# Edge lists loaded by GpSimd, counting one chunk sooner, and head 0 aggregated ahead of head 1's last chunk, in a two-block graph-attention kernel

## The reference

```python
edge_index = jnp.stack([src, dst])                       # 4096 edges among 256 nodes
x = _layernorm(x + _L0_gnn_ref(x, edge_index, ...))      # block 0: two GAT layers, 8 heads of 768, then 1 of 768
x = _layernorm(x + _L1_gnn_ref(x, edge_index, ...))      # block 1: two GAT layers, 4 heads of 256, then 1 of 768, with layer norms

# one GAT layer, self-loops appended to src and dst
h = (x @ W).reshape(n, heads, out_ch)
e = leaky_relu(alpha_src[src] + alpha_dst[dst], 0.2)     # alpha = <h, a> of each head
p = exp(e - segment_max(e, dst)[dst])
alpha = p / segment_sum(p, dst)[dst]
out = segment_sum(h[src] * alpha, dst) + b
```

## Time and profile before

| | |
|---|---|
| median of 3 runs | 353.04 us (353.0, 353.04, 353.94) |
| the profiled execution | 353.03 us |
| its span in the profile | 351.2 us |
| PE busy with matmuls | 343.7 us, 98% |
| DVE, ACT, POOL busy | 214.4 us (61%), 219.0 us (62%), 249.4 us (71%) |
| chain that ended last | PE 93%, DVE 4%, DMA 1% |

### The profile page before, as it was taken

How to read it: one execution, slowest core, us unless ns; L and a number is a source line. 1 busy time by engine, 2 the same in 40 slices (tenths; PEclk the granted TensorE clock), 3 DMA queues, 4 the chain that set the end, 5 groups by cost and what they waited for, 6 DMA issues and landing times.

```text
span 351.2 us, 6049 instructions
## 1 busy us (share of the span) xinstructions
PE 343.7 (98%) x2049; PEld 297.0 (85%) x2051; DVE 214.4 (61%) x543; ACT 219.0 (62%) x383; POOL 249.4 (71%) x165
## 2 busy tenths in 40 slices
PE   7999999999999999999999999999999999999994
PEld 4888989889988988988898898889777888888883
DVE  4999873354527327354541834464797899964776
ACT  5988597547736854773775486479585865444601
POOL 2479769576693965769397486959757899697911
PEclk9999999999999999999999999999999999999999
DMA  8887968475747547575754757654563557355002
GB/s 256 302 303 214 404 214 264 178 207 163 233 131 238 158 135 239 135 242 145 213 179 136 223 179 240 212 179 145 171 202 104 204 177 216 119 174 184 2 0 90
DMA packets 24833, 65.95 MB, mean 188 GB/s; under 512 B 1984, under 2 KB 3056, under 8 KB 24816
## 3 DMA queue, kind: packets, MB, share of 16 engines
...
...
## 4 chain that ended last, share of the span: by engine, by line
PE 93%; DVE 4%; DMA 1%; issue 0%; ACT 0%; DVEq 0%
PE ps L1098 65%; PE ps L1200 10%; PE ps L1495 10%; PE ps L1550 2%; PE ps L1166 2%; DMA x_sb<-in_x 1%; PE ps L1293 1%; PE ps L1151 1%; DVE stats L1944 1%; PE ps L1229 1%; DVE ps L2201 1%; PE ps L1434 1%; DVE z L2208 1%; PE ps L1573 0%; PE ps L1251 0%
## 5 line engine op out<-in xcount | busy, mean ns | idle before, releaser
L401 POOL TENSOR_TENSOR ring_lo<-raw,ring_hi 128x768 fp32r<-128x768 f32 x92 | 167.2, 1851 | 65.1 <-ACT ring_hi L388 65.0
L388 ACT ACTIVATE ring_hi<-raw 128x768 fp32r<-128x768 f32 x96 | 77.3, 839 | 33.8 <-PE ps L1098 28.5
L1098 PE MATMUL ps<-ring_hi,zT_hi 128*128 128x256 f32 (+1 forms) x256 | 69.8, 345 | 0.0
L1098 PE MATMUL ps<-ring_lo,zT_hi 128*128 128x256 f32 (+1 forms) x256 | 67.8, 338 | 0.0
L1098 PE MATMUL ps<-ring_hi,zT_lo 128*128 128x512 f32 (+1 forms) x256 | 67.5, 338 | 0.0
L417 POOL TENSOR_TENSOR ring_lo<-raw,ring_hi 128x512 fp32r<-128x512 f32 (+1 forms) x40 | 59.4, 1519 | 10.3 <-ACT ring_hi L410 10.3
L1712 DVE CUSTOM_DVE_ANT_0 e<-ps,att 128x768 f32<-128x768 f32 x36 | 32.4, 954 | 46.7 <-PE ps L1098 46.7
L1098 PE MATMUL ps<-ring_hi,xT_hi 128*128 128x512 f32 (+1 forms) x192 | 51.2, 340 | 0.0
L1098 PE MATMUL ps<-ring_hi,xT_lo 128*128 128x512 f32 (+1 forms) x192 | 50.7, 337 | 0.0
L1098 PE MATMUL ps<-ring_lo,xT_hi 128*128 128x512 f32 (+1 forms) x192 | 50.5, 337 | 0.0
L1098 PEld LDWEIGHTS ps<-ring_lo,zT_hi 128*128 128x128 f32 x256 | 43.3, 188 | 5.6
...
## 6 DMA issues: line engine op xcount, KB each, us to landing
...
```

Source lines behind the costliest of these rows:

```text
L388: eng.activation(slot_hi(c), raw_chunk(c), ACT.Copy).then_inc(hi_done, 1)
L401: eng.tensor_tensor(slot_lo(c), raw_chunk(c), slot_hi(c).bitcast(F32), ALU.subtract)\
L1098: last = pe.matmul(ps[:, at + to:at + to + hi - lo], a, b[:, lo:hi], start=start and n == 0 and to != D, stop=stop and n == PASSES - 1, sk ...
```

## The change

Eight edits. (1) Both edge lists are loaded by DMAs of POOL's own queue, behind its `iota`, which now comes first there; SP no longer loads them. (2) `zeros` and `half` are set by DVE and not by POOL. (3) DVE makes the edge numbers and the five early ramps ahead of chunk 0's low part. (4) `count_edges` and `scores(0)` stand before chunk 1 of phase 1, `weights(0)` half-way through chunk 4, and `aggregate_T(0)` before chunk 5; ACT makes its last ramps sooner, ahead of the high parts of chunks 2 to 5. (5) The two clearing matmuls go: the first accumulating matmuls open the banks. (6) In head 0's ELU, DVE takes head 1's dots behind the second third, and ACT does the last two chunks of phase 2 and head 1's first h_hi ahead of the last third's zT_hi. (7) The transposes of x1 are handed over in parts of two and four blocks; the matmul on `zeros` behind them goes. (8) DVE centres the second part of y's tile 1 behind x1's first two low parts.

```diff
--- before.py
+++ after.py
@@ -220,8 +220,8 @@
         GAT2_NAT_AT = [2 * BANK, 0]
         GAT2_WT_AT = [3 * BANK + N, BANK + N]
         R2_AT = 4 * BANK
-        X1T_AT = [(3 * BANK, 2 * BANK), (5 * BANK, 6 * BANK)]
-        X1T_PARTS = [4, KD]
+        X1T_AT = [(2 * BANK, 3 * BANK), (6 * BANK, 5 * BANK)]
+        X1T_PARTS = [2, KD]
         H1_PART = KH // 2
         ELU_AT = [2 * BANK, 6 * BANK, 7 * BANK]
         AM_AT = [T_AT, S_AT + N]
@@ -605,8 +605,6 @@
 
             sp.dma_start(raw[:, 0, 0:D], w1[:, 0, 0, :]).then_inc(single_loaded[0], 16)
             sp.dma_start(raw[:, 0, D:2 * D], w1[:, 1, 0, :]).then_inc(raw_full[0], 16)
-            sp.dma_start(edges[:, 0, :], src.rearrange("(p t) -> p t", p=P)).then_inc(edges_loaded, 16)
-            sp.dma_start(edges[:, 1, :], dst.rearrange("(p t) -> p t", p=P)).then_inc(edges_loaded, 16)
             load_x(1)
             sp.dma_start(raw[:, 1, 0:D], w1[:, 2, 0, :]).then_inc(single_loaded[1], 16)
             load_x(2)
@@ -646,13 +644,13 @@
 
         @block.gpsimd
         def _(pool):
-            pool.memset(zeros[:, :], 0.0).then_inc(zeros_set, 1)
-            pool.memset(half[:, :], -0.5).then_inc(half_set, 1)
+            pool.iota(iota_i, pattern=[[1, 1 + N]], base=-1, channel_multiplier=0).then_inc(iota_ready, 1)
+            for n, ends_of in enumerate((src, dst)):
+                pool.dma_start(edges[:, n, :], ends_of.rearrange("(p t) -> p t", p=P)).then_inc(edges_loaded, 16)
             pool.memset(ident[:, :], 0.0).then_inc(consts, 1)
             pool.wait_ge(consts, 1)
             pool.affine_select(out=ident[:, :], in_=ident[:, :], compare_op=ALU.not_equal, fill=1.0,
                                base=0, pattern=[[-1, P]], channel_multiplier=1).then_inc(consts, 1)
-            pool.iota(iota_i, pattern=[[1, 1 + N]], base=-1, channel_multiplier=0).then_inc(iota_ready, 1)
             pool.memset(stats[:, :, :, 12:15], 0.0).then_inc(eps_set, 1)
             pool.wait_ge(eps_set, 1)
             for n, width in enumerate((D, HC, D, D)):
@@ -925,12 +923,10 @@
 
             for c in (0, 1):
                 split_hi(act, 1, c)
-            steps(10, 14)
+            steps(10, 17)
             projected_hi(0)
-            for c in (2, 3):
-                split_hi(act, 1, c)
-            steps(14, ACT_STEPS)
-            for c in (4, 5):
+            steps(17, ACT_STEPS)
+            for c in (2, 3, 4, 5):
                 split_hi(act, 1, c)
             act.wait_ge(counted, 1)
             act.activation(step_sums, ps[:, STEPS_AT:STEPS_AT + 1 + N], ACT.Copy).then_inc(sums_copied, 1)
@@ -952,10 +948,13 @@
                 split_hi(act, 2, c)
             weights_hi(0)
             act.wait_ge(b1_ready, 2)
-            elu(0, between=lambda: projected_after_dots(1, 0))
-            split_hi(act, 2, 4)
+            def behind_last_exp():
+                for c in (4, 5):
+                    split_hi(act, 2, c)
+                projected_after_dots(1, 0)
+
+            elu(0, between=behind_last_exp)
             leaks(1)
-            split_hi(act, 2, 5)
             projected_after_dots(1, 1)
             exps(1, (1, 0))
             after_exps(1)
@@ -1088,7 +1087,7 @@
             def pieces(i):
                 return ((0, BANK, 0), (BANK, D, BANK)) if i == 0 else ((0, N, D), (N, D, 2 * BANK))
 
-            def product(at, i, lhs_hi, lhs_lo, w_hi, w_lo, start, stop, piece=None, passes=ALL):
+            def product(at, i, lhs_hi, lhs_lo, w_hi, w_lo, start, stop, piece=None, passes=ALL, opens=False):
 
                 last = None
                 for n, (a, b) in enumerate(three(lhs_hi, lhs_lo, w_hi, w_lo)):
@@ -1096,7 +1095,7 @@
                         continue
                     for lo, hi, to in pieces(i) if piece is None else pieces(i)[piece:piece + 1]:
                         last = pe.matmul(ps[:, at + to:at + to + hi - lo], a, b[:, lo:hi],
-                                         start=start and n == 0 and to != D,
+                                         start=n == 0 and (opens or start and to != D),
                                          stop=stop and n == PASSES - 1, skip_group_check=True)
                 return last
 
@@ -1294,28 +1293,22 @@
                 last.then_inc(counted, 1)
 
             for c in range(CH):
-                if c == 2:
+                if c == 1:
                     pe.wait_ge(b1_ready, 2)
                     count_edges()
                     scores(0)
-                project_chunk(1, 1, c, between=(lambda: weights(0)) if c == CH - 1 else None)
-
-            def clear_acc(b):
-                pe.matmul(ps[:, ACC + b * BANK:ACC + (b + 1) * BANK], zeros[:, 0:P], zeros[:, :],
-                          start=True, stop=False, skip_group_check=True)
-
-            aggregate_T(0)
-            clear_acc(1)
-            clear_acc(2)
-
-            def first_accumulate(c, i, passes=ALL, piece=None, start=False):
+                if c == CH - 1:
+                    aggregate_T(0)
+                project_chunk(1, 1, c, between=(lambda: weights(0)) if c == CH - 2 else None)
+
+            def first_accumulate(c, i, passes=ALL, piece=None, start=False, opens=False):
                 return product(ACC, i, node_tile(zT_hi, c, i), node_tile(zT_lo, c, i), slot_hi(c), slot_lo(c),
-                               start, False, passes=passes, piece=piece)
+                               start, False, passes=passes, piece=piece, opens=opens)
 
             pe.wait_ge(z_hi_done, 1)
             for c in (0, 1):
                 chunk(2, c)
-                first_accumulate(c, 1, passes=FIRST_TWO)
+                first_accumulate(c, 1, passes=FIRST_TWO, opens=c == 0)
             pe.wait_ge(z_lo_done, 1)
             for c in (0, 1):
                 first_accumulate(c, 1, passes=LAST_ONE)
@@ -1481,7 +1474,6 @@
                         last.then_inc(x1T_ps, 1)
 
             transpose_x1(0)
-            keep_warm(1, PROJ)
 
             def wide_product(q, at, i, passes=ALL):
 
@@ -1521,7 +1513,7 @@
                 wide_product(q, 0, 0, passes=LAST_ONE)
             for i in range(NT):
                 for q in w1a[2:] if i == 0 else w1a:
-                    if i == 0 and q["k"] == X1T_PARTS[0]:
+                    if i == 0 and q["k"] == BANK // P:
                         transpose_x1(1)
                     if q["k"] == X1T_PARTS[0] or i == 1 and q["k"] == 0:
                         pe.wait_ge(x1T_lo_done, 2 * i + 1 + (q["k"] > 0))
@@ -1637,6 +1629,8 @@
                 dve.tensor_tensor(xT_lo[:, 2 * b:2 * b + 2, :], of, xT_hi[:, 2 * b:2 * b + 2, :].bitcast(F32),
                                   ALU.subtract).then_inc(xT_lo_done, 1)
 
+            dve.memset(zeros[:, :], 0.0).then_inc(zeros_set, 1)
+            dve.memset(half[:, :], -0.5).then_inc(half_set, 1)
             dve.wait_ge(iota_ready, 1)
             dve.tensor_copy(iota[:, :], iota_i).then_inc(iota_cast, 1)
             dve.tensor_copy(iota_ps, iota_i).then_inc(iota_cast, 1)
@@ -1656,8 +1650,6 @@
                     dve.tensor_scalar(hot(t), iota_ps[:, 1:1 + P], row_of[:, t:t + 1], weight_of[:, t:t + 1], ALU.is_equal, ALU.mult)\
                        .then_inc(hot_done, 1)
 
-            split_lo(dve, FIRST_PHASE, 0)
-            input_lo(0)
             dve.wait_ge(edges_loaded, 32)
             dve.tensor_copy(edges_f[:, :, :], edges[:, :, :]).then_inc(edges_cast, 1)
             dve.wait_ge(edges_cast, 1)
@@ -1674,10 +1666,12 @@
                     dve.tensor_scalar(step(t), numbers, edges_f[:, 0, t:t + 1], weight_of[:, t:t + 1],
                                       ALU.is_lt if t >= BELOW_FROM else ALU.is_ge, ALU.mult).then_inc(step_dve_done, 1)
 
-            split_lo(dve, FIRST_PHASE, 1)
             dve.wait_ge(iota_cast, 2)
             dve.wait_ge(edges_split, 5)
             late_steps(ACT_STEPS, ACT_STEPS + STEPS_EARLY)
+            split_lo(dve, FIRST_PHASE, 0)
+            input_lo(0)
+            split_lo(dve, FIRST_PHASE, 1)
             split_lo(dve, FIRST_PHASE, 2)
             input_lo(1)
             late_steps(ACT_STEPS + STEPS_EARLY, ET - STEPS_LAST)
@@ -1846,9 +1840,9 @@
             def elu(h, between=None):
 
                 for q in range(3):
-                    if q == 1 and between is not None:
+                    if q == 2 and between is not None:
                         between()
-                    if q >= 1:
+                    elif q >= 1:
                         elu_lo(h, q - 1)
                     dve.wait_ge(elu_exp, 3 * h + q + 1)
                     for c in range(2):
@@ -1909,10 +1903,14 @@
             normalised(FIRST_HEAD, (0, 1))
             projected_lo(0, 1)
             weights_lo(0)
-            dve.wait_ge(att_loaded, 32 * 2)
-            dots(1, a_s, 0, a_src_done)
-            dots(1, a_d, 1, a_dst_done, tiles=(0,))
-            elu(0, between=lambda: dots(1, a_d, 1, a_dst_done, tiles=(1,)))
+            def next_dots():
+                dve.wait_ge(att_loaded, 32 * 2)
```

(8 more changed lines are left out.)

## The result

The changed kernel takes **360.63 us** (median of 5 runs, 360.49 to 360.70) against 353.36 us of the kernel before in the same comparison (5 runs, 353.0 to 354.75): 1.020 times as long, 95% interval 1.018 to 1.022. The forecast was 353.1 us with a range up to 355.0, so it missed by 7.5 us, on the side of its rival (b).

The account below looks back on a forecast made before the run. PE, working in 98% of the span, was taken as the bound. Opening and counting +0.94, accumulation gap -0.49, head 1's dots +0.15 and x1 -0.55 gave +0.05, 353.1 us; expected within 352.2 and 354.0, full range 351.8 to 355.0.

Parts of the forecast that it names:

- rival (b): Opening: edges come late through slow descriptor writing by POOL, PE waits for the first low part; 355.0 us, chance 0.22.
- the landing time: Opening: POOL's edge loads land at 4.6 us, so PE goes on at 7.80 instead of 7.17, +0.63 us.
- late end: Opening: edges land no sooner than SP's second edge load, 4.7 us after an issue at 2.11: 6.8 us.
- delay of some tenths: Opening: DVE's memsets and casts, under 1 us in all, stretch POOL's edge issues by some tenths of a us.
- early end: Opening: after POOL's iota and two issues of about 0.4 us, edges land 2.3 us after issue: 3.8 us, costing PE nothing.
- Rival (c): First chunks, at x's arrival: PE runs at the lower clock, costing about 2.1 us, 355.1 us in all; chance 0.06.
- nothing for those: Counting sooner: ACT's last ramps are ready before PE needs them and POOL's low parts are ahead; no cost.
- the wait for `am`: Head 0's weights: PE asks 2.1 us sooner, DVE answers 0.94 us sooner, so a wait of 0.3 us appears.
- a delay of 0.63 in the opening: Opening: PE starts on chunk 0's low part at 7.80 and not at 7.17, behind the edge numbers and ramps.
- The gap at the accumulation, -0.49: Before head 0's accumulation: chunk 5 fills the gap where the clearing matmuls lay; removing those alone gives nothing.
- Head 1's dots, +0.15: Head 1's weights: dots after chunk 5 start ACT's leaks at A + 5.8, A being the accumulation's start; 0 to 0.5 us.
- x(1), -0.55: x1: smaller first part and `y_centre(1)` moved behind x_lo let PE start its first product sooner, 0.55 us gained.

Follow-up runs that it names:

- e13: The changed kernel, but ScalarE's queue loads the edges, behind x's first piece: 359.25 us, 1.017 times the kernel before.
- e12: The changed kernel, but the edges are SP's first two transfers, ahead of the weights: 355.22 us, 1.007 times the kernel before.
- e1: The changed kernel, but SP loads the edges behind the first two weight loads, as before: 358.70 us, 1.014 times the kernel before.
- e3: The changed kernel, but SP loads the edges and VectorE computes the first low parts where it did before: 355.64 us, 1.005 times the kernel before.
- e14: The changed kernel, but ScalarE copies head 0's weights ahead of its high parts of phase 2's chunks 2 and 3: 358.86 us, 1.015 times the kernel before.
- e6: e3, but ScalarE copies head 0's weights ahead of its high parts of phase 2's chunks 2 and 3: 353.99 us, 1.001 times the kernel before.
- e10: The kernel before with only the x(1) edits and without the two clearing products: 352.49 us, 0.998 times the kernel before.
- e9: e8, with head 1's dots and ScalarE's chunks 4 and 5 of phase 2 back where they were: 352.74 us, 1.000 times the kernel before.
- e8: e3, with head 0's aggregation back behind head 1's last chunk and its weights' transposes back inside that chunk: 354.11 us, 1.002 times the kernel before.
- e5: The kernel before with the x(1) edits alone: 352.67 us, 0.999 times the kernel before.
- e4: The kernel before with only GpSimd's two edge loads, behind the iota and ahead of its memsets: 354.57 us, 1.005 times the kernel before.

## Why the prediction was wrong

- **"I take 4.6, in the lower half, for SP's edges had two 384 KB loads ahead of them in their queue and POOL's have none."** This step failed: the landing time. The edges were cast at 8.12. The changed kernel itself, e13 and e12 show that another queue, an empty one too, does not help once the loads of the weights are under way (5.2 to 6.0 us to land), and that a place ahead of them does (1.8 and 2.7 us). The "late end" was no end either: SP's landing time was added to SP's issue, 6.8, and nothing excluded that a transfer issued at the same moment on another queue takes longer (5.2 to 6.0 us and not 4.7).
- **The price of a late landing.** Rival (b) had its place right: at 6.8 us it gave PE's pass at 9.99, and e1, which lands there, has 10.15. But it priced the whole at 355.0, and e1 takes 358.7. Missing were the lower pace behind the wait (from the pass to `b_rows` 5.81 us in e1, 4.03 before: 1.8 us) and the copy of the weights (its stretch 9.41, less the chunk 7.33, 1.06 over before, where the sum had 0.49 under).
- **GpSimd's issues.** The delay of some tenths that rival (b) allowed is what the rows have: they take 0.74 and 0.55 us, SP's 0.42 and 0.43. The second load is issued at 2.12, where the early end had it near 1.5. That is not what made the landing late; e13's, with 0.49 and 0.45 on ScalarE, took as long to land.
- **The clock.** The sum had no term for it behind a wait, and this is the third thing that failed. Rival (c) looked for the lower clock at x's arrival. In the changed kernel it came behind PE's wait for `ring_lo`, 4.2 us without work: the two cost 5.9 us together, where a sum by waiting alone gives 4.3. At x's arrival the slow start of e3 and others is what (c) describes, at 1.7 us where it said some 2.1; it is no part of the changed kernel's loss, whose profile starts quick.
- **"nothing for those", of ScalarE's reordered list.** The second failing step. For every producer of what PE asks for sooner the forecast had to work out when it is ready; it did so for `am` and not for `pT_hi`. It stood behind two high parts whose transfer SP issued at 33.57 in the changed kernel and 29.29 in e3, but at 27.05 before. It cost 2.0 us in the changed kernel (9.94 less e14's 7.94) and 1.6 in e3 (9.53 less e6's 7.94). By the traces the later issue alone would not have made ScalarE wait; the landing, 7.7 us instead of 4.2 behind two loads of `att` that the sooner counting put ahead of it, does.
- **Counting sooner and the wait for `am`.** Right: PE asks 2.1 us sooner, VectorE answers less than that sooner, and a wait of 0.3 us was forecast. The row says 0.45; without the late edges, in e3, the longest is 0.4, where 0.9 was said. So the 0.3 was met partly by luck: it was worked out as the part of 0.9 that a delay of 0.63 in the opening leaves, and the wait is the same with a delay of 6 us and with far less.
- **The gap at the accumulation, -0.49.** Right: -0.41 once `pT_hi` is out of the way (e6, e14), and nothing from taking the clearing alone (e10).
- **Head 1's dots, +0.15.** Right: ScalarE begins head 1's leaks at A + 5.83, where A + 5.8 was said, and the stretch grew by 0.35, within the 0 to 0.5 given. e9 against e8 shows that it is edit (6).
- **x(1), -0.55.** The stretch to the first product gave 0.44, and 0.44 more came by the end of the span; in e5 the latter is 0.28, and e4, which has not the edit, has 0.17 of it, so how much belongs to the edit is not settled.

As a sum: waiting +4.3, clock +1.6, `am` and `pT_hi` +0.3 and +2.0, gap -0.4, dots +0.35, x(1) and behind it -0.9, which is +7.25 of the span's 7.3.
